# A two-layer attention-bias kernel in ten regions of rows instead of eleven, with other store and load pieces

## The chip, the cores and the metric

The kernel runs on one core of a Trainium2 chip. The metric is the device time of one execution in microseconds (us). Lower is better. The engines are called as in the profile: PE (TensorE), DVE (VectorE), ACT (ScalarE), POOL (GpSimd) and SP (SyncE, which here only issues DMAs).

## The reference

The input x has 16 heads of 1024 rows (t) by 1024 columns (s), all float32. The output has the same shape. Two layers are applied one after the other:

```python
x = x + bias.transpose(2, 0, 1)[None]                 # bias[t, s, head]
ret = einsum('BGMTS,GMN->BGNTS', x, w + eye)
ret += einsum('BGITS,BTGIM->BGMTS', einsum('BGMTS,BTGIM->BGITS', x, qw1), qw2)
ret += einsum('BGMTS,BSGIM->BGITS', x, kw1) followed by kw2
ret += x * qdd (by row and head) + x * kdd (by column and head)
```

The bias is a small network of the distance of row and column: a logarithm of the distance, divided by one of the row's position, goes through 32 hidden units with a relu and then through a 32 x 16 matrix. In the second layer the 16 heads of each point (t, s) are mixed by a 16 x 16 matrix that is the sum of a part that depends on the row t ("a", from w, qw1, qw2, qdd) and a part that depends on the column s ("b", from kw1, kw2, kdd).

## The kernel before

The 1024 rows are cut into 128 tiles of 8 rows. A tile holds all 1024 columns and all 16 heads: 8 blocks of 128 columns by 16 heads make the 128 partitions, and each partition has 8 x 128 = 1024 numbers, so a tile is 512 KB. Tiles are grouped into regions (`REGION_TILES`): one of 6 tiles, nine of 13, one of 5, eleven in all. The text calls them region 0 to region 10. SBUF has three "homes" of 13 tiles each. The biased x of region k lies in home k mod 3, and its mixed output goes into the home behind it in that ring ((k + 2) mod 3), from which it is stored. The x of region k + 2 is loaded into the home of region k's output, one tile further on, and so each piece of that load waits until the store of the tiles lying there is out (`out_done`). The last tile of a region's load falls into the first tile of the next home and waits for the first store piece there.

A region has two phases on PE. First come 16 column steps (`b_columns`, L772): each takes 8 columns of every block and multiplies all rows of the region by the column's matrices. A step has 16 matmuls with 64 x 64 weights and as many columns as the region has rows (104 for 13 tiles). For regions of up to 8 tiles (`NARROW_TILES`) a step has 32 matmuls with 32 x 32 weights instead (48 or 40 columns). ACT and DVE copy the sums out of PSUM (`take_b`, L528 and L641) in turn, in region 0 ACT alone; PSUM holds two such steps. Then come the row tiles (`a_rows`, L759), one for each tile of the region, with 16 matmuls of 128 columns each; DVE adds their results to the copied sums (`finish_tile`, L651). Each matmul of an order is two instructions in the trace.

Between these steps the bias of the NEXT region is made, one tile at a time, spread evenly over the steps from step 4 on (`bias_step`). For a tile POOL makes the hidden values (L462), ACT the relu (L501), PE the product (`bias_tile`, L789), and DVE (L677, L671) and ACT (L512) add it to x, for which they wait for the load of that tile's piece (`x_landed`). In the first 64 tiles this takes one pass of POOL and ACT for each tile; in the last 64 it takes two. The text calls regions 1 to 3 light and regions 4 to 8 heavy (in region 4 half of the next region's tiles take two passes). POOL also spreads the row matrices of each tile out into the weights that PE needs (L439), in a ring of four tiles. They come from `mats_in`, which SP loads for four tiles at a time (`load_mats_a`, L333).

Before region 0 the kernel loads its constants, makes the bias of region 0's own tiles, builds the column matrices on DVE (`compact("b")`) and sends them through DRAM into `mats_b`. After the last tile of that bias DVE builds the row matrices (`compact("a")`, L298 to L606), PE transposes them after the fourth column step (`TURN_AT`), and SP writes them to DRAM and reads them back (L359, L333). A table of scales for later rows goes to DRAM, too (`late_scales`, L380). The scratch for all this lies in parts of the homes that are not yet used, so some loads have to come after it.

SP issues all loads and half of the stores from one queue, in an order that is written out in the program: in region k, at tile T, first the row matrices that are due, then the last piece of x for region k + 1, then the store piece that ends there (waiting until DVE has finished its last tile), then a piece of x for region k + 2 (at T = 7, 10 and 12). The remaining pieces for region k + 1 stand at the start of region k. ACT issues the other half of the stores, in two portions at the two steps after a piece's last tile. Each piece of a load or of a store is one DMA for each of the 8 blocks (8 loads on SP; 4 stores on SP and 4 on ACT). The pieces are in `LOAD_PIECES` and `STORE_PIECES`, in tiles.

## Time and profile before

| | us |
|---|---|
| median of 3 runs | 897.41 (889.36 to 899.29) |
| the profiled execution | 896.75 |
| its span, from the first to the last instruction | 894.9 |
| around the span | 1.85 |
| mean granted TensorE clock | 0.894 |

Engine times of the page are sums over the span, and a share of busy time says little where the stages have different limits. The stages are best read from windows that are cut at the first column step of each region; the timeline gives these times, 46.3 us for region 0 and 839.2 us for region 10 being the first and the last.

### The profile page before, as it was taken

Reading aid. Unit: us, or ns where it says so; the run is one execution under the profiler, and the core shown is the slowest. Engines: PE = TensorE matmul, PEld = TensorE weight load, DVE = VectorE, ACT = ScalarE, POOL = GpSimd, SP = SyncE. Lnnn points to the kernel's source line nnn. Section 1 sums busy time; section 2 is a strip of 40 time slices with the busy share of each in tenths; the row PEclk is TensorE's granted clock in tenths of the full one; section 3 lists DMA queues with packets and bytes.
Section 4 is the critical chain, followed back from the end, with each engine's and each line's share of the span. In section 5 each row is a group of like instructions: output and inputs, shape, how many; then the busy total and the mean of one; then the engine's idle time right before and its main releaser. Section 6 shows DMA issues by size and latency. Waiting matters only on the chain. (4 is left out here: it accounts for less than half of the span.)

```text
span 894.9 us, 28881 instructions
## 1 busy us (share of the span) xinstructions
PE 699.0 (78%) x12836; PEld 586.1 (65%) x12836; DVE 481.0 (54%) x629; ACT 395.8 (44%) x428; POOL 513.4 (57%) x463
## 2 busy tenths in 40 slices
PE   0466767986998798696699859969988896699764
PEld 0254566875887688585577657756866685589664
DVE  7667625863693595475346625653475365335412
ACT  5756536544743663563245325433543453232000
POOL 4524823734475257368558937985898588635300
PEclk9876978988998899899899979998999999799857
DMA  6578559597778979877885888589859897843905
GB/s 129 137 169 147 132 145 205 128 227 169 181 185 208 208 149 223 213 159 150 189 195 125 201 185 188 113 185 215 183 123 184 180 198 151 212 111 73 258 7 118
DMA packets 302936, 148.98 MB, mean 166 GB/s; under 512 B 31964, under 2 KB 298588, under 8 KB 302812
## 3 DMA queue, kind: packets, MB, share of 16 engines
q1 hardware_dynamic: 232928, 113.56, 57.5%
q10 hardware_dynamic: 69884, 33.58, 16.3%
q8 instruction: 101, 1.65, 0.8%
q14 instruction: 23, 0.19, 0.1%
HBM read 77.61 MB, written 69.47 MB: 164 GB/s over the span
## 5 line engine op out<-in xcount | busy, mean ns | idle before, releaser
L462 POOL TENSOR_TENSOR hidden<-log_table,row_scale 128x1024 f32<-128x1024 f32 x192 | 364.3, 1913 | 218.3 <-PE bias L789 210.4
L772 PEld LDWEIGHTS main<-homes,mats_b 64*64 64x64 f32 (+1 forms) x6656 | 316.9, 189 | 150.3 <-ACT homes L528 65.1
L772 PE MATMUL main<-homes,mats_b 64*64 64x104 f32 (+2 forms) x6656 | 332.5, 274 | 106.1 <-ACT homes L528 50.7
L501 ACT ACTIVATE hidden<-hidden,b_col 128x1024 f32<-128x1024 f32 x192 | 221.0, 1152 | 259.6 <-POOL hidden L462 187.6
L759 PEld LDWEIGHTS main<-homes,mats_a 64*64 64x64 f32 x4096 | 239.2, 136 | 51.3 <-issue 37.4
L759 PE MATMUL main<-homes,mats_a 64*64 64x128 f32 x4096 | 256.0, 279 | 5.2 <-POOL mats_a L439 3.5
L439 POOL TENSOR_TENSOR mats_a<-mats_in,own_block 128x256 f32<-128x256 f32 x256 | 153.6, 655 | 143.0 <-DMA mats_in<-a_mats 112.9
L651 DVE TENSOR_TENSOR homes<-main,homes 128x1024 f32<-128x1024 f32 x128 | 156.7, 1225 | 59.4 <-PE main L759 54.3
L641 DVE COPY homes<-main 128x832 f32<-128x832 f32 (+1 forms) x80 | 77.7, 971 | 192.1 <-PE main L772 189.2
L789 PE MATMUL bias<-hidden,w_blocks 64*32 64x256 f32 (+1 forms) x2048 | 120.4, 528 | 58.0 <-ACT hidden L501 46.4
L677 DVE SCALAR_TENSOR_TENSOR homes<-bias,b_col,homes 64x256 f32<-64x256 f32 x256 | 122.9, 480 | 76.7 <-DMA homes<-in_x 52.8
L528 ACT ACTIVATE homes<-main 128x832 f32<-128x832 f32 (+2 forms) x96 | 73.4, 764 | 141.2 <-PE main L772 125.9
L671 DVE SCALAR_TENSOR_TENSOR homes<-bias,b_col,homes 128x512 f32<-128x512 f32 x128 | 90.3, 747 | 68.0 <-PE bias L789 58.2
L512 ACT ACTIVATE homes<-homes,b_col 64x512 f32<-64x512 f32 x128 | 89.9, 754 | 63.5 <-DMA homes<-in_x 52.3
L789 PEld LDWEIGHTS bias<-hidden,w_blocks 64*32 64x32 f32 x2048 | 24.8, 108 | 79.4 <-issue 60.2
L298 DVE TENSOR_TENSOR homes<-homes 128x2048 f32<-128x2048 f32 x4 | 12.3, 3123 | 0.1
L719 PE MATMUL bias<-relu_b,w_blocks 64*32 64x1 f32 x4 | 0.3, 191 | 13.7 <-DVE w_blocks L626 13.7
L719 PEld LDWEIGHTS bias<-relu_b,w_blocks 64*32 64x32 f32 x4 | 0.2, 136 | 13.6 <-issue 13.6
L495 ACT ACTIVATE mats_b<-zero_col 128x8192 f32<-128x8192 f32 x1 | 7.0, 7012 | 0.0
L712 PE MATMUL main<-homes 128*128 128x128 f32 x32 | 5.6, 350 | 0.6 <-DVE homes L606 0.6
L712 PEld LDWEIGHTS main<-homes 128*128 128x128 f32 x32 | 5.0, 183 | 1.5 <-issue 0.8
L601 DVE TENSOR_TENSOR homes<-homes 128x2048 f32<-128x2048 f32 x2 | 4.6, 2292 | 0.1
(40 smaller groups left out, 33.0 us busy)
## 6 DMA issues: line engine op xcount, KB each, us to landing
homes<-in_x SPq DMA_DIRECT2D x224, 192.0 KB, 6.2
out_mixed<-homes SPq DMA_DIRECT2D x108, 192.0 KB, 4.8
out_mixed<-homes ACTq DMA_DIRECT2D x108, 192.0 KB, 5.4
out_mixed<-homes SPq DMA_DIRECT2D x88, 128.0 KB, 3.5
out_mixed<-homes ACTq DMA_DIRECT2D x88, 128.0 KB, 3.6
homes<-in_x SPq DMA_DIRECT2D x160, 64.0 KB, 4.4
homes<-in_x SPq DMA_DIRECT2D x80, 128.0 KB, 4.5
mats_in<-a_mats SPq DMA_DIRECT2D x128, 64.0 KB
```

The source lines that it names most:

```text
L439: spread_half = nc.gpsimd.tensor_tensor(bass.AP(mats_a, w % A_RING_UNITS * A_UNIT + q * GP, [[A_RING_UNITS * A_UNIT, P], [GS, H], [1, GS], ...
L462: nc.gpsimd.tensor_tensor(hidden_tile(u, g).rearrange("p (j b s) -> p j b s", b=2, s=W), bass.AP(log_table, t0 - SLOTS * W * g, [[2 * TABL ...
L501: nc.scalar.activation(hidden_tile(u, g), hidden_tile(u, g), ACT.Relu, bias=b1_col[:, 0:1])\
L512: add = nc.scalar.activation(y_rows(high_half, k, T, b), x_rows(high_half, k, T, b), ACT.Identity, bias=b2_col[high_half, 1:2])
L528: nc.scalar.activation(mixed_columns(k, C), column_sums(k, C), ACT.Copy)\
L641: dve.tensor_copy(mixed_columns(k, C), column_sums(k, C)).then_inc(main_taken[b_tile(k, C) % 2], 1)
L651: dve.tensor_tensor(at, main[:, i % 2, :], at, ALU.add).then_inc(main_taken[i % 2], 1)
L671: add = dve.scalar_tensor_tensor(out=y_rows(whole, k, T, b), in0=falling(u, b), scalar=b2_col[:, 0:1], in1=x_rows(whole, k, T, b), op0=ALU ...
L677: add = dve.scalar_tensor_tensor(out=y_rows(low_half, k, T, b)[:, some], in0=falling_part(u, part, b), scalar=b2_col[low_half, 0:1], in1=x ...
L759: mm = pe.matmul(main[of_wide(g), i % 2, j * W:(j + 1) * W], a_weights(g, w, j), y_row(k, T, g, j), start=True, stop=True)
L772: mm = pe.matmul(main[at, i % 2, j * W:j * W + REGION_TILES[k] * ROWS], b_weights(at, C * ROWS + j), y_column(k, at, C * ROWS + j), start= ...
L789: mm = pe.matmul(bias[quadrant(q), u % 2, b * BANK:b * BANK + n * W], w2_blocks[of, :], rows[:, b, part * n:(part + 1) * n, :], start=True ...
```

## The change

The regions become one of 11 tiles and nine of 13, so there are ten, region 0 to region 9. With 11 tiles region 0 takes the wide column steps, and no region takes the narrow ones. A full region's stores go out in six pieces of 1, 2, 3, 3, 2, 2 tiles instead of five of 2, 3, 3, 3, 2, and the last region has a list of its own. The x of a full region comes in pieces of 1, 2, 3, 3, 3, 1 tiles instead of 1, 3, 3, 3, 2, 1. The scratch moves into other parts of the homes, and the order of SP's start changes with it. DVE makes the late scales one bias tile sooner.

```diff
+SCRATCH_FROM = 9
-REGION_TILES = (6,) + (13,) * 9 + (5,)
+REGION_TILES = (11,) + (13,) * 9
...
-STORE_PIECES = {6: (2, 2, 2), 13: (2, 3, 3, 3, 2), 5: (2, 1, 1, 1)}
-STORE_SEMS = max(len(sizes) for sizes in STORE_PIECES.values())
-LOAD_PIECES = {6: (1, 2, 3), 13: (1, 3, 3, 3, 2, 1), 5: (1, 4)}
+STORE_PIECES = {11: (2, 3, 3, 3), 13: (1, 2, 3, 3, 2, 2)}
+LAST_STORES = (2, 3, 3, 2, 1, 1, 1)
+STORE_SEMS = len(LAST_STORES)
+LOAD_PIECES = {11: (1, 2, 4, 4), 13: (1, 2, 3, 3, 3, 1)}
...
-            return STORE_PIECES[REGION_TILES[k]]
+            return LAST_STORES if k == REGIONS - 1 else STORE_PIECES[REGION_TILES[k]]
+
+        def loads_ahead(k):
+
+            return len(load_pieces(k)) - (REGION_TILES[k] == HOME_TILES)
...
             for i in range(3):
                 load_x(1, i)
             save_mats("a")
-            load_x(1, 3)
             sp.wait_ge(mats_out["a"], 2 * DMA)
             for v in range(A_RING):
                 load_mats_a(v)
-            load_x(1, 4)
             sp.wait_ge(tables_made, 3)
             sp.dma_start(late_scales, scale_late).then_inc(scales_out, DMA)
-            loaded = [3, 5] + [0] * (REGIONS - 2)
+            sp.wait_ge(scales_out, DMA)
+            for i in range(3, loads_ahead(1)):
+                load_x(1, i)
+            loaded = [loads_ahead(0), loads_ahead(1)] + [0] * (REGIONS - 2)
...
-                        if T == piece_start(store_pieces(k), i + 1) - 1 - (i == 4 and k < REGIONS - 1):
+                        if T == piece_start(store_pieces(k), i + 1) - 1 - (REGION_TILES[k] == HOME_TILES and i == len(store_pieces(k)) - 1 and k < REGIONS - 1):
                             store_upper(k, i)
...
-                    if k == 0 and T == 3:
+                    if k == 0 and T == 2:
                         invert(scale_late)
```

Three places show how instructions move. In a row, the last numbers before the count are the shape; for loads and stores 16x8x128 is one tile of one block, 16x24x128 is three tiles, and a count of 8 (loads) or 4 (stores) is one piece.

SP at the start, from the first load of region 1's x on, before:

```order
L325 DMA homes<-in_x 16x8x128 x8
L325 DMA homes<-in_x 16x24x128 x16
L359 DMA a_mats<-homes 128x32x32 x2
L325 DMA homes<-in_x 16x24x128 x8
L333 DMA mats_in<-a_mats 32x1x512 x8
L325 DMA homes<-in_x 16x16x128 x8
L380 DMA late_scales<-homes 128x512
L276 DMA out_mixed<-homes 16x16x128 x4
```

and now:

```order
L332 DMA homes<-in_x 16x8x128 x8
L332 DMA homes<-in_x 16x16x128 x8
L332 DMA homes<-in_x 16x24x128 x8
L366 DMA a_mats<-homes 128x32x32 x2
L340 DMA mats_in<-a_mats 32x1x512 x8
L385 DMA late_scales<-homes 128x512
L332 DMA homes<-in_x 16x24x128 x16
L283 DMA out_mixed<-homes 16x16x128 x4
```

The two pieces of x that hold tiles 6 to 11 of region 1 now stand behind the late scales, and wait until these have landed in DRAM.

SP in a full light region, at the same phase of the row matrices (region 2 before), from its first store on:

```order
L276 DMA out_mixed<-homes 16x16x128 x4
L333 DMA mats_in<-a_mats 32x1x512 x4
L276 DMA out_mixed<-homes 16x24x128 x4
L325 DMA homes<-in_x 16x8x128 x8
L333 DMA mats_in<-a_mats 32x1x512 x4
L276 DMA out_mixed<-homes 16x24x128 x4
L325 DMA homes<-in_x 16x8x128 x8
L276 DMA out_mixed<-homes 16x24x128 x4
L325 DMA homes<-in_x 16x24x128 x8
L333 DMA mats_in<-a_mats 32x1x512 x4
L276 DMA out_mixed<-homes 16x16x128 x4
L325 DMA homes<-in_x 16x24x128 x16
```

and now (region 1):

```order
L283 DMA out_mixed<-homes 16x8x128 x4
L283 DMA out_mixed<-homes 16x16x128 x4
L340 DMA mats_in<-a_mats 32x1x512 x4
L283 DMA out_mixed<-homes 16x24x128 x4
L332 DMA homes<-in_x 16x8x128 x8
L340 DMA mats_in<-a_mats 32x1x512 x4
L332 DMA homes<-in_x 16x8x128 x8
L283 DMA out_mixed<-homes 16x24x128 x4
L283 DMA out_mixed<-homes 16x16x128 x4
L332 DMA homes<-in_x 16x16x128 x8
L340 DMA mats_in<-a_mats 32x1x512 x4
L283 DMA out_mixed<-homes 16x16x128 x4
```

Ahead of the first one-tile load (the last tile of the next region) there are now 12 stores and 6 stored tiles instead of 8 and 5. The second piece of x for the region after that has 2 tiles instead of 3 and comes behind 20 stores instead of 16; the third piece, of 3 tiles, follows the last row shown in both.

PE at the end of the program, before:

```order
L789 MATMUL bias<-hidden,w_blocks 32x512 x8
L759 MATMUL main<-homes,mats_a 64x128 x96
L789 MATMUL bias<-hidden,w_blocks 32x512 x8
L759 MATMUL main<-homes,mats_a 64x128 x16
L772 MATMUL main<-homes,mats_b 32x40 x512
L759 MATMUL main<-homes,mats_a 64x128 x80
L67 UNCONDITIONAL_BRANCH
```

and now:

```order
L767 MATMUL main<-homes,mats_a 64x128 x32
L797 MATMUL bias<-hidden,w_blocks 32x512 x8
L767 MATMUL main<-homes,mats_a 64x128 x16
L780 MATMUL main<-homes,mats_b 64x104 x256
L767 MATMUL main<-homes,mats_a 64x128 x208
L69 UNCONDITIONAL_BRANCH
```

The narrow region of 512 small matmuls and 5 row tiles at the end is gone; the program now ends with a full region of 16 wide column steps and 13 row tiles with no bias between them.

## Rows read from the trace of the kernel before

**Rows 1.** The page, part 1: busy time, share of the span, instructions.

```profile
PE 699.0 (78%) x12836; PEld 586.1 (65%) x12836; DVE 481.0 (54%) x629; ACT 395.8 (44%) x428; POOL 513.4 (57%) x463
```

**Rows 2.** Windows: stretch, length, busy PE, PEld, DVE, ACT, POOL, clock, DMA, GB/s.

```profile
46.30:119.70 73.40, 45.63 (x1442) 35.02 (x1442) 46.29 (x68) 42.38 (x57) 35.95 (x33) 0.78 0.71 150
119.70:350.30 230.60, 199.62 (x3409) 176.78 (x3409) 144.84 (x220) 119.48 (x141) 115.62 (x114) 0.90 0.82 185
350.30:771.50 421.20, 352.04 (x5682) 285.05 (x5684) 214.33 (x247) 182.64 (x177) 304.53 (x252) 0.94 0.80 176
518.30:609.80 91.50, 71.94 (x1140) 58.01 (x1138) 42.44 (x47) 37.25 (x36) 68.48 (x58) 0.91 0.79 169
771.50:839.20 67.70, 60.81 (x1012) 55.21 (x1008) 31.13 (x31) 17.52 (x18) 30.96 (x33) 0.92 0.62 143
839.20:894.90 55.70, 30.83 (x1186) 29.07 (x1184) 11.28 (x14) 3.50 (x8) 4.72 (x8) 0.65 0.43 99
```

**Rows 3.** Timeline, start of the program (start, length, engine, line, idle before).

```profile
39.49 1.11 PE L789 MATMUL bias<-hidden,w_blocks 64*32 64x256 f32 x16 [1.47 <-ACT hidden L501]
...
42.88 4.49 DVE L298 TENSOR_TENSOR homes<-homes 128x2048 f32<-128x2048 f32 x2
...
46.26 4.55 PE L772 MATMUL main<-homes,mats_b 32*32 32x48 f32 x231 [5.66 <-DMA mats_b<-b_mats]
...
52.06 0.37 DVE L606 TENSOR_TENSOR homes<-homes 128x128 f32<-128x128 f32 x1
...
54.70 1.12 PE L772 MATMUL main<-homes,mats_b 32*32 32x48 f32 x64 [0.24 <-ACT homes L520]
```

**Rows 4.** DMA issues by line: count, KB of each, median us to landing.

```profile
homes<-in_x SPq DMA_DIRECT2D x224, 192.0 KB, 6.2
out_mixed<-homes SPq DMA_DIRECT2D x108, 192.0 KB, 4.8
...
a_mats<-homes SPq DMA_DIRECT2D x2, 512.0 KB, 10.9
out_mixed<-homes SPq DMA_DIRECT2D x12, 64.0 KB, 2.4
...
late_scales<-homes SPq DMA_DIRECT2D x1, 256.0 KB, 4.6
```

**Rows 5.** The page, part 5: groups of instructions (busy, mean ns of one, idle before).

```profile
L462 POOL TENSOR_TENSOR hidden<-log_table,row_scale 128x1024 f32<-128x1024 f32 x192 | 364.3, 1913 | 218.3 <-PE bias L789 210.4
...
L677 DVE SCALAR_TENSOR_TENSOR homes<-bias,b_col,homes 64x256 f32<-64x256 f32 x256 | 122.9, 480 | 76.7 <-DMA homes<-in_x 52.8
```

**Rows 6.** Timeline, region 10 and the end.

```profile
866.21 2.36 PE L772 MATMUL main<-homes,mats_b 32*32 32x40 f32 x128 [1.12 <-issue]
...
870.80 11.73 PE L759 MATMUL main<-homes,mats_a 64*64 64x128 f32 x160
...
882.58 1.23 DVE L651 TENSOR_TENSOR homes<-main,homes 128x1024 f32<-128x1024 f32 x1 [0.59 <-PE main L759]
```

**Rows 7.** Timeline, region 2: a stall, column steps, row tiles.

```profile
221.69 5.81 PE L772 MATMUL main<-homes,mats_b 64*64 64x104 f32 x64 [8.28 <-ACT homes L528]
...
228.03 3.77 PE L772 MATMUL main<-homes,mats_b 64*64 64x104 f32 x64
...
262.84 3.85 PE L759 MATMUL main<-homes,mats_a 64*64 64x128 f32 x64
```

**Rows 8.** Timeline of SP, early in region 3.

```profile
295.34 20.39 SPq L325 DMA_DIRECT2D homes<-in_x  x24
```

**Rows 9.** Timeline, the start of region 6 (518.3 us).

```profile
524.47 2.34 POOL L439 TENSOR_TENSOR mats_a<-mats_in,own_block 128x256 f32<-128x256 f32 x4 [8.51 <-DMA mats_in<-a_mats]
```

**Rows 10.** Waits of ACT and of PE, 119.7 to 434.2 and 350.3 to 771.5 us.

```profile
ACT homes L512 <- DMA homes<-in_x: 39.5, 8, 8.9
...
PE bias L789 <- ACT hidden L501: 39.0, 25, 5.0
PE main L772 <- ACT homes L528: 24.6, 3, 9.0
```

More of the change, by code:

```diff
@@ L95, in build @@
         thr_col = sb("thr_col", [P, 3])
-        spare_0 = homes[:, (REGION_TILES[0] + 1) * COLS:HOME_TILES * COLS]
-        spare_2 = homes[:, (2 * HOME_TILES + REGION_TILES[0]) * COLS:HOMES * HOME_TILES * COLS]
-        comp = {"a": spare_2[:, 0:2048], "b": spare_2[:, 2048:4096]}
-        term = {"a": spare_0[:, 0:2048], "b": spare_2[:, 4096:6144]}
-        turned = term
-        first = {"a": spare_2[:, 6144:6400], "b": spare_2[:, 6400:6656]}
-        second = {"a": spare_2[:, 6656:6912], "b": spare_2[:, 6912:7168]}
-        diag = {"a": spare_0[:, 2048:2176], "b": spare_0[:, 2176:2304]}
-        w_eye = spare_0[:, 2304:2560]
-        ident = spare_0[:, 2560:2688]
-        w2_rows = spare_0[:, 2688:2704]
-        own_halves = spare_0[:, 2704:2704 + GROUPS * GS]
-        scale_late = spare_0[:, 2816:2816 + PART]
+        spare_1 = homes[:, (HOME_TILES + SCRATCH_FROM) * COLS:2 * HOME_TILES * COLS]
+        home_2 = homes[:, 2 * HOME_TILES * COLS:HOMES * HOME_TILES * COLS]
+        spare_2 = home_2[:, REGION_TILES[0] * COLS:HOME_TILES * COLS]
+        comp = {"a": spare_2[:, 0:2048], "b": home_2[:, 0:2048]}
+        term = {"a": spare_1[:, 0:2048], "b": home_2[:, 2048:4096]}
+        turned = term
+        first = {"a": spare_1[:, 2048:2304], "b": home_2[:, 4096:4352]}
+        second = {"a": spare_1[:, 2304:2560], "b": home_2[:, 4352:4608]}
+        diag = {"a": spare_1[:, 2560:2688], "b": home_2[:, 4608:4736]}
+        w_eye = spare_1[:, 2688:2944]
+        ident = spare_1[:, 2944:3072]
+        w2_rows = spare_1[:, 3072:3088]
+        own_halves = spare_1[:, 3088:3088 + GROUPS * GS]
+        scale_late = spare_1[:, 3104:3104 + PART]
         main = ctx.enter_context(nc.psum_tensor("main", [P, 2, COLS], F32))
@@ L364, in _ @@
             sp.dma_start(w_eye, w.rearrange("g m n -> g (m n)").partition_broadcast(P)).then_inc(weights_in["a"], DMA)
-            load_x(0, 1)
-            load_x(0, 2)
+            for i in range(1, loads_ahead(0)):
+                load_x(0, i)
             save_mats("b")
@@ L377, in _ @@
                 load_mats_a(v)
-            load_x(1, 4)
             sp.wait_ge(tables_made, 3)
             sp.dma_start(late_scales, scale_late).then_inc(scales_out, DMA)
-            loaded = [3, 5] + [0] * (REGIONS - 2)
+            sp.wait_ge(scales_out, DMA)
+            for i in range(3, loads_ahead(1)):
+                load_x(1, i)
+            loaded = [loads_ahead(0), loads_ahead(1)] + [0] * (REGIONS - 2)
             for k in range(REGIONS):
-                while k + 1 < REGIONS and loaded[k + 1] < min(5, len(load_pieces(k + 1))):
+                while k + 1 < REGIONS and loaded[k + 1] < loads_ahead(k + 1):
                     load_x(k + 1, loaded[k + 1])
@@ L397, in _ @@
                         load_mats_a(v)
-                    if k + 1 < REGIONS and len(load_pieces(k + 1)) > 5 and T == min(6, REGION_TILES[k] - 4):
-                        load_x(k + 1, 5)
+                    if k + 1 < REGIONS and REGION_TILES[k + 1] == HOME_TILES and T == min(6, REGION_TILES[k] - 4):
+                        load_x(k + 1, loads_ahead(k + 1))
                     for i in range(len(store_pieces(k))):
-                        if T == piece_start(store_pieces(k), i + 1) - 1 - (i == 4 and k < REGIONS - 1):
+                        if T == piece_start(store_pieces(k), i + 1) - 1 - (REGION_TILES[k] == HOME_TILES and i == len(store_pieces(k)) - 1 and k < REGIONS - 1):
                             store_upper(k, i)
                     if k + 2 < REGIONS and (T in AHEAD or k == 0 and T == REGION_TILES[0] - 1) \
-                            and loaded[k + 2] < len(load_pieces(k + 2)):
+                            and loaded[k + 2] < loads_ahead(k + 2):
                         load_x(k + 2, loaded[k + 2])
```

## The prediction

> **What bounds the kernel now.** The page comes first. No engine is full: PE, the busiest, works for 78% of the span [rows 1], so the time must be read by stages. For that I cut the span where the timeline shows each region's first column step, and asked for the windows [rows 2]. The reader should divide length by tiles. Start-up takes 46.3 us. Region 0 takes 73.4 us for 6 tiles, regions 1 to 3 take 230.6 for 39, regions 4 to 8 take 421.2 for 65, region 9 takes 67.7 for 13, and region 10, with the last stores, 55.7 for 5. These six add up to the span of 894.9. A tile costs 5.2 to 7.0 us in a full region, but 12.2 in region 0 and 11.1 in region 10. The short regions are dear, because 16 column steps are done however many rows share them.
>
> What a step costs is read from the timeline. Two wide steps (64 instructions) take 3.77 us, 1.885 each, and two row tiles 3.85, 1.925 each [rows 7]. Two narrow steps of region 10 take 2.36, 1.18 each, but then 1.12 pass in which PE waits for nothing the profile names [rows 6]; with such pauses its column phase lasts from 839.2 to 870.8, 31.6 us. Sixteen wide steps are 16 x 1.885 = 30.2. So 5 tiles pay as much for columns as 13 do.
>
> Then the waits. In the light regions ACT and DVE wait for x that has not landed: ACT loses 39.5 us in 8 such waits between 119.7 and 434.2 [rows 10], and one of them holds PE for 8.28 us in region 2 [rows 7]. In the heavy regions POOL is late, because the row matrices land late: 8.51 us at the start of region 6 [rows 9]. PE then waits for the hidden values, 39.0 us in 25 waits, and for ACT's copies, 24.6 us in 3 [rows 10]. SP issues both kinds of load from one queue, so both waits hang on how far SP lags behind PE.
>
> **The end.** Region 10 goes, and the last region has 13 tiles and no bias beside it. Columns: 30.2 us, plus 2 for ACT, which issues two stores of the region before ahead of its first copy (an estimate: two issues of 0.85 [rows 8]). Rows: 13 x 1.925 = 25.0. The tail after PE's last row tile was 894.9 - 882.5 = 12.4 [rows 2, 6]; the last store pieces were 2, 1, 1, 1 tiles and are still 2, 1, 1, 1, so I keep it. Sum 69.6, where regions 9 and 10 took 123.4 together.
>
> **The start.** Eleven tiles of bias stand ahead of region 0 instead of six. PE's sixth came at 39.49 after 1.47 us idle, so one tile takes 1.47 + 1.11 = 2.58 [rows 3]. The eleventh comes at 39.5 + 5 x 2.58 = 52.4. From the sixth to the start of the row matrices on DVE 3.4 us passed (42.88 - 39.49), so region 0 can start at about 55.8. Before, it waited for the column matrices until 46.26 [rows 3]; they queue behind five more tiles of x now, 2.5 MB, but have 9.5 us more to land. If they take longer still, the start slips by as much.
>
> DVE needs 52.43 - 42.88 = 9.55 us for the row matrices, and from their end to the next column step 2.3 us passed [rows 3]: column step 4 starts at 67.7. Twelve wide steps of 88 columns are at most 12 x 1.885 = 22.6, and seven bias tiles lie between them. The seventh needs tile 6 of region 1, whose load now stands behind the row matrices and the late scales. That chain: matrices out at 68.7, landed 10.9 later [rows 4], read back in about 6 (8 issues), 86; scales out, 4.6 [rows 4] and the issue, 92; 8 loads and 6.2 to land [rows 4], about 102. DVE makes these scales after the third bias tile now, at column step 7 (before after the fourth, at step 8). They are ready when the matrices are read back, so this move saves nothing here, and at most the wait for one bias addition. ACT holds PE until 104, some 8 us later than its own work would. From there DVE has 10 row tiles of 1.23 [rows 6] and six bias additions of 4 x 0.48 = 1.92 [rows 5], and one of each is left over from the wait: 27 us, and the one-tile load behind the fourth row tile's store ends at the same time. Region 1 starts at 132. Bounds: 124 without the wait, 142 if every load is as late as a_mats was. Before it was 119.7, so five tiles cost 12.3 us more.
>
> **The full light regions (1 to 3).** Their work does not change; the pieces do. Each has four more stores on SP and four more on ACT. Issues cost 20.39 / 24 = 0.85 us in the busy stretch [rows 8], so four are 3.4. Against this the first store starts a row tile sooner (about 2.5), when SP is waiting for it. The second piece of x has a third fewer bytes and so lands up to 2.5 us sooner, but the third piece now begins with tile 3 instead of tile 4. That tile is used two steps and a bias tile earlier, over 2 x 1.885 = 3.8 us, while its piece lands 1 us later to 2.6 sooner. The wait at tile 1 becomes a wait at tile 3. Bounds: the waits vanish (8.28 off in region 2), or 5 us come on top in each. I take 2 each, since the queue is the same and the last data that a step needs come no sooner: 230.6 + 6 = 236.6.
>
> A rule of the Trainium skill speaks against such pieces. The rows show 2.4 us to landing for a store DMA of 64 KB and 4.8 for one of 192 KB [rows 4], which is 1.2 per 64 KB and 1.2 that does not shrink. The Trainium skill ("DMA: Bandwidth & Descriptors", section "Anatomy of one DMA") states a fixed part of about 2.0 us for each DMA, and "Measured" there advises batches of 1 MiB. Were 2.0 paid once more in each of the nine full regions, the sum would be 18 us higher; the trace has the next issue 0.85 behind, beside that latency.
>
> **The heavy regions (4 to 8).** There are still five, and 64 tiles with two passes, but region 4 now has 12 of them to make instead of 7. POOL's second pass is 1.91 us [rows 5], so this costs 0 to 9.5; I take 5, since half of the region is bound by POOL. Row matrices due at tiles 7, 9, 10 and 11 stand behind four more stores, 0 to 3.4 each; they delay POOL only where it already waits. I take 4 for all. 421.2 + 9 = 430.2. Bounds: 2 less in each if the earlier first store helps, or all as long as region 6, 91.5 [rows 2].
>
> **Sum.** 132.0 + 236.6 + 430.2 + 69.6 = 868.4, plus the 1.85 around the span: 870.3, called 870. The profiled execution took 896.75 and the median of the runs is 897.41, so both stand for the same; 870 is 3.0% less.
>
> **Rivals.**
>
> *The finer pieces dissolve the waits for x (0.13).* The second piece lands in time and the third as well. For it: the first store leaves sooner, while SP stands idle. Against it: the third piece holds a tile that is needed sooner. ACT's waits of 39.5 us lie in about four regions [rows 10], 9.9 in each, and PE, which runs two steps ahead, loses less. Were 6 saved in each light region instead of 2 lost, the time would be 870 - 24 = 846.
>
> *The pieces cost what the short region gives (0.20).* Each region pays in series: the light ones 5 instead of 2, the heavy ones 3.4 each, 17 instead of 4. That is 9 + 13 more: 892, no change. For it: SP lags PE already, and the DMA engines are 0.80 to 0.82 busy in these stretches [rows 2]. Against it: the bytes are the same. The rule of the Trainium skill above would end here, at 888.
>
> *The row matrices come late in every heavy region (0.10).* Region 6, with its wait, took 91.5 us; the other four average (421.2 - 91.5) / 4 = 82.4 [rows 2]. If four more issues ahead of `load_mats_a` put all five regions there and add 3.4, they take 5 x 94.9 = 474.5 instead of 430.2: 870 + 44 = 914, slower. For it: the matrices are asked for only about two row tiles ahead of their use. Against it: the matrices fall due at another tile in each region, and only some of these lie behind more stores than before. It decides once the matrices land later than those two row tiles, about 6 us, in each region.
>
> **How the numbers follow.** My forecast has 0.57, with a range of its own of 856 to 884 (the start's bounds, 2 us per light region either way). A measurement of this kernel can tell about 1% from no change, here 888 to 906. Faster by more: 0.56 + 0.13, and a third of the 0.20, 0.75. Within 1%: the rest of it, 0.14. Slower: 0.10 and a little, 0.11. The range of 846 to 896 leaves out the slower rival and about half of the first.
>
> **What would show it.** Right: no PE instructions with 32 x 32 weights for columns; region 1 starting between 124 and 142; the last region, with the tail, at 67 to 73; the light regions' waits for x moved from tile 1 to tile 3. Wrong: region 1 later than 145 (the start pays for what the end saves), heavy regions of 90 or more with POOL waiting for `mats_in` longer than before (the third rival), or light regions under 72 (the first).

## The result and the profile after

The changed kernel took 860.77 us (median of 4 runs, 859.05 to 868.05), the kernel before, beside it, 898.35 (889.36 to 902.84). One of its four runs, that of 902.84, counts as slow, and the ratio leaves it out. The ratio is 0.963, with a 95% interval of 0.953 to 0.973: 3.7% faster. The forecast was 870 with a range of 846 to 896. The profiled execution took 861.78, of which 860.0 is the span and 1.78 lies around it.

The page, part 1, of the kernel after, against [rows 1]:

```profile
PE 680.8 (79%) x11300; PEld 574.0 (67%) x11300; DVE 474.9 (55%) x621; ACT 395.4 (46%) x420; POOL 512.9 (60%) x463
```

PE has 1536 instructions less. A narrow region's 16 column steps are 1024 instructions, a wide region's 512; two narrow regions go and one wide comes. But PE's work fell by 18.2 us only, and the span by 34.9: about half of the gain was not PE's work. In the rows shown line numbers are 8 higher than before for the computing engines (column steps L780, row tiles L767, bias product L797), and 7 higher for SP (store L283, load of x L332, row matrices L340).

The windows of the kernel after, cut as in [rows 2] (stretch, length, busy PE, PEld, DVE, ACT, POOL, clock, DMA, GB/s):

```profile
0.00:57.20 57.20, 14.34 (x198) 5.53 (x198) 39.38 (x70) 42.89 (x44) 31.12 (x29) 0.82 0.71 153
57.20:141.10 83.90, 63.65 (x1088) 55.74 (x1088) 53.41 (x75) 46.35 (x57) 41.79 (x43) 0.89 0.73 160
141.10:384.30 243.20, 199.35 (x3408) 175.99 (x3408) 144.88 (x220) 119.99 (x142) 114.59 (x112) 0.89 0.79 179
384.30:791.00 406.70, 350.67 (x5680) 284.56 (x5682) 211.86 (x237) 179.23 (x171) 313.42 (x259) 0.96 0.80 181
791.00:860.00 69.00, 52.81 (x932) 52.14 (x928) 25.34 (x22) 6.91 (x8) 11.98 (x20) 0.92 0.58 138
```

Read down the lengths. Start-up and region 0 now take 141.1 us instead of 119.7. The light regions take 243.2 instead of 230.6, the heavy ones 406.7 instead of 421.2, and the end 69.0 instead of 67.7 + 55.7 = 123.4. That is +21.4, +12.6, -14.5 and -54.4, in sum -34.9. The second number of a row, PE's work, hardly moved in the light and heavy regions (199.62 to 199.35, 352.04 to 350.67). What changed there is time in which PE stood still: 31.0 to 43.9 us and 69.2 to 56.0.

The end, in the timeline of the kernel after, against [rows 6]:

```profile
791.00 3.79 PE L780 MATMUL main<-homes,mats_b 64*64 64x104 f32 x64
...
796.12 25.23 PE L780 MATMUL main<-homes,mats_b 64*64 64x104 f32 x448 [1.32 <-ACT homes L536]
...
821.18 16.48 PE L767 MATMUL main<-homes,mats_a 64*64 64x128 f32 x288
...
839.39 7.47 PE L767 MATMUL main<-homes,mats_a 64*64 64x128 f32 x128 [1.73 <-POOL mats_a L447]
```

The columns take 821.18 - 791.00 = 30.2 us with the wait of 1.32, the 13 row tiles 25.7 (821.18 to 846.86) with the wait of 1.73, and 13.1 remain for the last stores.

The start, in the timeline of PE, ACT and DVE:

```profile
105.32 1.37 ACT L520 ACTIVATE homes<-homes,b_col 64x512 f32<-64x512 f32 x2 [9.12 <-DMA homes<-in_x]
...
107.61 5.83 PE L767 MATMUL main<-homes,mats_a 64*64 64x128 f32 x64 [8.73 <-ACT homes L536]
...
139.09 1.97 DVE L685 SCALAR_TENSOR_TENSOR homes<-bias,b_col,homes 64x256 f32<-64x256 f32 x4 [8.45 <-DMA homes<-in_x]
...
141.12 1.14 PE L780 MATMUL main<-homes,mats_b 64*64 64x104 f32 x10 [9.23 <-DVE homes L685]
```

There are two stalls. Tile 6 of region 1 arrives at 105.3, and PE stands still for 8.73 us. The region's last tile, the one-tile piece, arrives at 139.1, and PE stands still for 9.23. SP's queue in the same stretch says why:

```profile
112.58 3.60 SPq L283 DMA_DIRECT2D out_mixed<-homes  x4
116.22 3.16 SPq L340 DMA_DIRECT2D mats_in<-a_mats  x4
121.00 4.66 SPq L283 DMA_DIRECT2D out_mixed<-homes  x4
125.70 4.55 SPq L340 DMA_DIRECT2D mats_in<-a_mats  x4
130.30 5.74 SPq L332 DMA_DIRECT2D homes<-in_x  x8
```

The last row is the one-tile load. Right ahead of it stand row matrices, 4.55 us of issues, and ahead of these a store, for which SP had waited until 121.00, when DVE was done with tile 4.

The light regions, in PE's own timeline of regions 1 to 3, against [rows 7] (the rows of regions 1 and 2 with a stall on x inside the region):

```profile
166.36 5.00 PE L780 MATMUL main<-homes,mats_b 64*64 64x104 f32 x64 [6.92 <-ACT homes L536]
...
242.27 4.70 PE L780 MATMUL main<-homes,mats_b 64*64 64x104 f32 x64 [6.43 <-ACT homes L536]
256.98 5.56 PE L780 MATMUL main<-homes,mats_b 64*64 64x104 f32 x64 [5.12 <-ACT homes L536]
```

Where region 2 had one stall of 8.28 us [rows 7], it has two now, 6.43 for the second piece of x (tile 1) and 5.12 for the third (tile 3); region 3 likewise has 4.58 and 3.62.

The waits of SP and of PE in the heavy regions (384.3 to 791.0), against [rows 10]. Each row gives the wait in sum, how many times it came, and the longest. Of before, the first of these waits was 56.9 us in 10 times (its row stands with the experiments):

```profile
SPq L283 <- DVE homes L659: 39.9, 12, 10.9
...
PE bias L797 <- ACT hidden L509: 38.5, 29, 3.7
...
PE main L780 <- ACT homes L536: 16.4, 4, 8.6
```

SP waits for DVE 17 us less, though it has more stores to wait for. This is not idle time of the bottleneck, but everything queued behind such a wait goes out later, and that is what the experiments are about.

### The profile page after: what moved, and what is told of

The parts are those of the page before. It is cut to its first block and busy times, and to the rows that moved or that the text cites. A ratio compares the mean times of both kernels' runs of the same rounds, so it can differ in the third digit from the quotient of the medians.

```text
span 860.0 us, 25839 instructions
## 1 busy us (share of the span) xinstructions
PE 680.8 (79%) x11300; PEld 574.0 (67%) x11300; DVE 474.9 (55%) x621; ACT 395.4 (46%) x420; POOL 512.9 (60%) x463
## 5 line engine op out<-in xcount | busy, mean ns | idle before, releaser
L780 PEld LDWEIGHTS main<-homes,mats_b 64*64 64x64 f32 x5120 | 308.9, 204 | 107.2 <-ACT homes L536 62.8
L780 PE MATMUL main<-homes,mats_b 64*64 64x104 f32 (+1 forms) x5120 | 320.8, 283 | 68.1 <-ACT homes L536 44.7
L767 PEld LDWEIGHTS main<-homes,mats_a 64*64 64x64 f32 x4096 | 236.0, 134 | 59.5 <-issue 46.9
L767 PE MATMUL main<-homes,mats_a 64*64 64x128 f32 x4096 | 252.6, 277 | 17.3 <-ACT homes L536 8.7
L797 PE MATMUL bias<-hidden,w_blocks 64*32 64x256 f32 (+1 forms) x2048 | 117.0, 514 | 65.4 <-ACT hidden L509 54.9
L649 DVE COPY homes<-main 128x832 f32<-128x832 f32 x72 | 73.7, 1024 | 148.6 <-PE main L780 148.3
L536 ACT ACTIVATE homes<-main 128x832 f32<-128x832 f32 (+1 forms) x88 | 73.6, 840 | 97.5 <-PE main L780 96.3
L797 PEld LDWEIGHTS bias<-hidden,w_blocks 64*32 64x32 f32 x2048 | 24.8, 107 | 89.7 <-issue 63.2
L305 DVE TENSOR_TENSOR homes<-homes 128x2048 f32<-128x2048 f32 x4 | 12.3, 3122 | 0.1
L727 PEld LDWEIGHTS bias<-relu_b,w_blocks 64*32 64x32 f32 x4 | 0.2, 136 | 13.6 <-issue 13.6
L528 ACT ACTIVATE homes<-main 128x1024 f32<-128x1024 f32 x4 | 3.9, 1021 | 1.9 <-PE main L720 1.9
```

The source lines that it names most:

```text
L536: nc.scalar.activation(mixed_columns(k, C), column_sums(k, C), ACT.Copy)\
L649: dve.tensor_copy(mixed_columns(k, C), column_sums(k, C)).then_inc(main_taken[b_tile(k, C) % 2], 1)
L767: mm = pe.matmul(main[of_wide(g), i % 2, j * W:(j + 1) * W], a_weights(g, w, j), y_row(k, T, g, j), start=True, stop=True)
L780: mm = pe.matmul(main[at, i % 2, j * W:j * W + REGION_TILES[k] * ROWS], b_weights(at, C * ROWS + j), y_column(k, at, C * ROWS + j), start= ...
L797: mm = pe.matmul(bias[quadrant(q), u % 2, b * BANK:b * BANK + n * W], w2_blocks[of, :], rows[:, b, part * n:(part + 1) * n, :], start=True ...
```

## Experiments

All ratios are to the kernel before, run beside each on the same chip. The names of the kernels say what they hold: ten or eleven regions, and old or new pieces of stores and loads. "The changed kernel" and "after" are the same.

### Regions and pieces apart

Ten regions with both old lists:

```diff
-STORE_PIECES = {11: (2, 3, 3, 3), 13: (1, 2, 3, 3, 2, 2)}
+STORE_PIECES = {11: (2, 3, 3, 3), 13: (2, 3, 3, 3, 2)}
-LOAD_PIECES = {11: (1, 2, 4, 4), 13: (1, 2, 3, 3, 3, 1)}
+LOAD_PIECES = {11: (1, 2, 4, 4), 13: (1, 3, 3, 3, 2, 1)}
```

> Ten regions with the old pieces in the full regions (stores 2, 3, 3, 3, 2; loads 1, 3, 3, 3, 2, 1). Theory 'regions': the smaller number of regions carries the whole gain and the new pieces cost a little in the light regions; then the light regions fall from 243 back to about 231 us, the heavy ones stay near 407, and the time is about 848 to 855. Theory 'pieces': the heavy regions are shorter because of the new pieces; then they go back to 421 to 430 us, and the time is 865 to 875. Theory 'phases': the heavy regions are shorter because the row matrices fall due at other tiles now that region 0 has 11 tiles; then they stay near 407 with either pieces, and only the light ones tell the pieces apart.

Measured: 859.60 us (858.36 to 863.32), ratio 0.962 (0.957 to 0.967).

Only the first of the two lines (old stores, new loads):

> Ten regions, new loads (1, 2, 3, 3, 3, 1), old stores (2, 3, 3, 3, 2). Theory 'regions' or 'phases': four stores fewer on SP per region ahead of the second piece of x; light regions 235 to 240 us, time 853 to 860. Theory 'pieces': the one-tile first store is what frees SP earlier, so without it the time is above 865.

Measured: 863.47 (861.14 to 868.51), ratio 0.966 (0.960 to 0.973).

Only the second (new stores, old loads):

> Ten regions, new stores (1, 2, 3, 3, 2, 2), old loads (1, 3, 3, 3, 2, 1). If the new loads cost in the light regions, because their third piece begins a tile sooner, the time falls by 3 to 8 us under 861; if they help, because the second piece lands sooner, it rises to 865 to 870.

Measured: 859.14 (855.56 to 874.01), ratio 0.959 (0.953 to 0.965).

The kernel before with the new pieces in its full regions:

```diff
-STORE_PIECES = {6: (2, 2, 2), 13: (2, 3, 3, 3, 2), 5: (2, 1, 1, 1)}
+STORE_PIECES = {6: (2, 2, 2), 13: (1, 2, 3, 3, 2, 2), 5: (2, 1, 1, 1)}
-LOAD_PIECES = {6: (1, 2, 3), 13: (1, 3, 3, 3, 2, 1), 5: (1, 4)}
+LOAD_PIECES = {6: (1, 2, 3), 13: (1, 2, 3, 3, 3, 1), 5: (1, 4)}
...
-if T == piece_start(store_pieces(k), i + 1) - 1 - (i == 4 and k < REGIONS - 1):
+if T == piece_start(store_pieces(k), i + 1) - 1 - (i == 5 and k < REGIONS - 1):
```

> The kernel before with its eleven regions, and the new pieces in its full regions. Theory 'regions': no gain, 895 to 905 us (my sum: 6 us more in the light and 4 more in the heavy regions). Theory 'pieces': the heavy regions fall by some 15 us as they did with the whole change, and the time is 880 to 888. Theory 'phases': the heavy regions stay near 421.

Measured: 890.65 (887.69 to 894.28), ratio 0.996 (0.993 to 0.999).

The stages of all of these and of the later ones, from the timelines (first column step of each region), in us of the profiled execution:

| kernel | region 1 starts | regions 1 to 3 | regions 4 to 8 | from region 9 on |
|---|---|---|---|---|
| before | 119.7 | 230.6 | 421.2 | 123.4 |
| eleven_new_both | 118.4 | 233.9 | 412.0 | 121.9 |
| ten_old_both | 137.6 | 237.9 | 414.1 | 68.5 |
| ten_old_stores | 143.2 | 237.6 | 412.8 | 67.9 |
| ten_old_loads | 141.4 | 240.6 | 405.9 | 68.6 |
| after | 141.1 | 243.2 | 406.7 | 69.0 |
| after_again | 141.8 | 239.3 | 406.3 | 68.0 |
| two_three | 140.8 | 243.3 | 418.1 | 68.2 |
| first_two | 142.2 | 234.7 | 407.2 | 68.0 |
| first_two_again | 142.1 | 232.3 | 405.1 | 68.6 |
| first_two_old_loads | 139.1 | 232.9 | 412.5 | 68.3 |
| early_last | 133.7 | 249.9 | 408.3 | 71.0 |
| split_start | 144.8 | 238.9 | 405.2 | 69.3 |
| early_split | 136.1 | 245.8 | 402.4 | 70.8 |

What follows: the new regions alone carry the whole gain (0.962 with old pieces, 0.963 with new). The pieces alone are worth 0.4% in eleven regions and nothing that can be told in ten. A stage moves by up to 4 us between two profiles of one kernel (the two rows of the changed kernel), so only differences beyond that count. By this the cost of the pieces in the light regions is not shown (3.3 us in eleven regions, 5.3 or 1.4 in ten, by which profile of the changed kernel is taken), and their gain in the heavy ones is (9.2 in eleven, 7.4 or 7.8 in ten). Of the two lists it is the stores that do it: with old stores the heavy regions take 413 to 414, with the new ones 406 to 407, whichever loads go with them. (With the stores 2, 2, 3, 2, 2, 2 further down the loads do seem to matter there, 412.5 against 407.2 and 405.1.)

None of the theories came as it was put. The time of ten_old_both lies above what 'regions' gave and below 'pieces', and its heavy regions take 414.1, neither 407 nor 421; eleven_new_both is faster than 'regions' and slower than 'pieces' gave; ten_old_stores and ten_old_loads fall between their alternatives. The heavy regions gain about 7 us by the new regions and 7 to 9 by the stores.

One rival is untested. With the short regions the narrow column steps went, too, and in the kernel before PE stood 13.9 us in region 0 and 12.1 in region 10 in pauses inside those steps (the last section shows where they come from). No run keeps eleven regions and gives the short ones wide steps, so how much of the gain comes from one region less, and how much from the narrow steps, is not told apart.

The waits of SP in the heavy regions, before, in eleven regions with new pieces, and in ten with old ones, a row from each:

```profile
SPq L276 <- DVE homes L651: 56.9, 10, 10.1
```

```profile
SPq L276 <- DVE homes L651: 36.3, 11, 7.9
```

```profile
SPq L283 <- DVE homes L659: 57.3, 10, 13.7
```

With old stores SP waits 57 us for DVE, with new ones 36 and 40, in ten regions as in eleven. PE's own waits do not say as plainly where the gain arrives: between the old and new pieces of ten regions PE's wait for the hidden values falls from 43.0 to 38.5, between those of eleven it is the wait for ACT's copies that falls, from 24.6 to 19.0.

### The stall at the start

Theory: the one-tile load comes late because it stands behind what is due by tile 6, so issued earlier it would bring region 1 forward, and the whole kernel with it. Rival: SP sets the pace for regions 0 and 1 together, and what is won at region 1 is lost again at region 2.

```diff
-if k + 1 < REGIONS and REGION_TILES[k + 1] == HOME_TILES and T == min(6, REGION_TILES[k] - 4):
+if k + 1 < REGIONS and REGION_TILES[k + 1] == HOME_TILES and T == (2 if k == 0 else 6):
```

> The changed kernel with one move: in region 0 SP issues the last one-tile piece of region 1's x at tile 2 instead of tile 6. It removes most of PE's wait of 9.2 us ahead of region 1. Theory 'SP's order of work sets the pace': the second piece of region 2's x lands no sooner, since SP has the same loads and stores ahead of it, and PE waits for it longer in region 1; region 1 starts 6 to 8 us sooner, region 2 starts within 2 us of where it did, and the time stays at 859 to 862. Theory 'every wait of PE counts': the time falls by 6 to 8 us, to 853 to 855.

Measured: 863.30 (861.12 to 865.19), ratio 0.961 (0.956 to 0.965). Region 1 did start earlier. From the timeline of early_last, the starts of regions 1 and 2 and the stall between:

```profile
133.70 9.19 PE L780 MATMUL main<-homes,mats_b 64*64 64x104 f32 x160 [1.28 <-DVE homes L685]
...
165.98 5.21 PE L780 MATMUL main<-homes,mats_b 64*64 64x104 f32 x64 [9.24 <-ACT homes L536]
...
218.29 3.91 PE L780 MATMUL main<-homes,mats_b 64*64 64x104 f32 x64 [1.19 <-DVE homes L685]
```

and of the changed kernel, the start of region 2:

```profile
218.28 10.04 PE L780 MATMUL main<-homes,mats_b 64*64 64x104 f32 x160 [2.79 <-DVE homes L685]
```

The stall of 9.23 us shrank to 1.28, and region 1 began 7.4 us sooner. Region 2 began where it had, to 0.01 us. In between the wait at tile 1 grew from 6.92 to 9.24, since its piece still comes at SP's own time, and PE waited 4.84 us for DVE's copies at 152.79, where the changed kernel has no such wait. SP issues without a stop from 121.0 to 181.0 us in the changed kernel and from 121.2 to 179.9 in early_last; that piece is among these loads. The rival holds.

The other stall at the start, for tile 6, was attacked by splitting region 1's pieces otherwise and sending four of them ahead of the row matrices:

```diff
+return (1, 2, 3, 2, 4, 1) if k == 1 else LOAD_PIECES[REGION_TILES[k]]
...
-for i in range(3):
+for i in range(4):
     load_x(1, i)
 save_mats("a")
```

> The changed kernel with region 1's x in pieces of 1, 2, 3, 2, 4, 1 tiles. The fourth piece (tiles 6 and 7) then lies ahead of the scratch and is issued before the row matrices go out, instead of behind the late scales. PE's wait of 8.7 us in region 0 for tile 6 goes or moves to tile 8. The first store of region 0 leaves sooner, and SP's whole queue with it, so both theories expect a gain: 4 to 7 us, 854 to 857, if tile 8's piece lands in time; none if it lands as late as tile 6's did (106 us) and the wait is 6 us or more there.

Measured: 863.68 (860.14 to 866.25), ratio 0.962 (0.957 to 0.968). From its timeline, PE in region 0 and the start of region 1:

```profile
120.81 3.68 PE L767 MATMUL main<-homes,mats_a 64*64 64x128 f32 x32 [11.78 <-POOL mats_a L447]
...
144.85 10.78 PE L780 MATMUL main<-homes,mats_b 64*64 64x104 f32 x160 [8.49 <-DVE homes L685]
```

The stall for tile 6 is gone, and a longer one stands in its place: row matrices now hold PE for 11.78 us. They are issued at 114.8, in the changed kernel at 116.2: SP has no stop from 100.4 until they are out at 117.4 and can't send them much sooner, and PE is there earlier. Neither theory's gain came. Both edits together:

> Both moves. Theory 'SP's order': the same as split_start alone, within 2 us. Theory 'every wait of PE counts': the sum of the two, 845 to 850.

Measured: 862.05 (856.88 to 865.64), ratio 0.959 (0.953 to 0.965). Three orders of the start end within 3 us of each other and of the changed kernel, and region 2 starts at 218.3, 221.6 and 219.3 in their profiles (218.3 and 218.4 in the two of the changed kernel). This fits a start that is set by how much SP has to send, where the order only picks the engine that shows it. No run takes DMAs off SP in this stretch, so that much is a reading and not shown.

### Which property of the new stores pays

The new list differs from the old in a first store of one tile, in one piece more, and in where its pieces end. The first theory was that the one-tile store wakes SP sooner. A list with a first store of two tiles tells it apart:

```diff
-STORE_PIECES = {11: (2, 3, 3, 3), 13: (1, 2, 3, 3, 2, 2)}
+STORE_PIECES = {11: (2, 3, 3, 3), 13: (2, 2, 3, 2, 2, 2)}
```

> The changed kernel with six store pieces of 2, 2, 3, 2, 2, 2 tiles in full regions: as many stores, but the first is of two tiles and so leaves SP one row tile later. Theory 'the one-tile first store wakes SP sooner': in the heavy regions SP's waits for DVE go back from 40 to about 57 us, the row matrices due at tiles 8 and 9 are issued 11 us or more after they are due instead of 7 to 9, and regions 4 to 8 take 412 to 418 us instead of 407. Theory 'smaller pieces': they stay near 407.

Measured: 855.13 (853.97 to 855.24), ratio 0.951 (0.947 to 0.955). The theory falls: the heavy regions stay at 407, and the light ones give back 8.5 us (why is open). SP's waits for DVE in the heavy regions did go back in part, to 46.0 us, and the heavy regions did not follow. The next theories: smaller pieces pay as such, or what counts is which tile's store is the last ahead of the row matrices. (2, 3, 2, 2, 2, 2) has six pieces like the new list but ends its second at tile 4, as the old one does:

```diff
-STORE_PIECES = {11: (2, 3, 3, 3), 13: (1, 2, 3, 3, 2, 2)}
+STORE_PIECES = {11: (2, 3, 3, 3), 13: (2, 3, 2, 2, 2, 2)}
```

> Ten regions, new loads, six store pieces of 2, 3, 2, 2, 2, 2 tiles. SP's first two store pieces are as before the change, so after the last store for which SP has to wait for DVE (tile 4) it has 24 issues ahead of the row matrices due at tile 8, as with the old stores; with 2, 2, 3, 2, 2, 2 it has these 24 too, but waits last at tile 3. Theory 'what is queued behind SP's last wait': the matrices due at tile 8 of region 4 are issued 10 us or more after they are due, regions 4 to 8 take 411 to 415 us, and the time is about 860 to 864. Theory 'smaller pieces': they are issued about 7 us after, the heavy regions stay near 407, and the time is 854 to 857.

Measured: 870.21 (863.87 to 872.33), ratio 0.970 (0.964 to 0.975). Six pieces, and the heavy regions take 418.1, more than with the old five. So smallness is not it. The queue of SP in region 4, up to the row matrices due at tile 8 (the last row of each), shows what differs. With the old stores in ten regions:

```profile
425.96 2.55 SPq L340 DMA_DIRECT2D mats_in<-a_mats  x4
431.98 4.74 SPq L283 DMA_DIRECT2D out_mixed<-homes  x4
436.76 5.79 SPq L332 DMA_DIRECT2D homes<-in_x  x8
442.60 3.92 SPq L283 DMA_DIRECT2D out_mixed<-homes  x4
446.56 6.63 SPq L332 DMA_DIRECT2D homes<-in_x  x8
453.23 2.84 SPq L340 DMA_DIRECT2D mats_in<-a_mats  x4
```

In the changed kernel:

```profile
435.08 3.39 SPq L340 DMA_DIRECT2D mats_in<-a_mats  x4
439.93 2.87 SPq L283 DMA_DIRECT2D out_mixed<-homes  x4
442.84 13.03 SPq L332 DMA_DIRECT2D homes<-in_x  x16
455.91 3.14 SPq L340 DMA_DIRECT2D mats_in<-a_mats  x4
```

In first_two:

```profile
425.73 7.61 SPq L283 DMA_DIRECT2D out_mixed<-homes  x8
433.39 3.39 SPq L340 DMA_DIRECT2D mats_in<-a_mats  x4
436.82 5.12 SPq L332 DMA_DIRECT2D homes<-in_x  x8
441.99 3.68 SPq L283 DMA_DIRECT2D out_mixed<-homes  x4
445.71 6.29 SPq L332 DMA_DIRECT2D homes<-in_x  x8
452.04 2.50 SPq L340 DMA_DIRECT2D mats_in<-a_mats  x4
```

All three send 12 stores of this region ahead of these matrices (the first four or eight, at 423.36 and 427.78, stand above the rows shown); the number is the same. With the old stores SP stops at 428.51 (425.96 + 2.55) until tile 4 is done, 3.5 us, and then has 24 DMAs to issue, 21.3 us, among them the store that ends at tile 7. In the changed kernel the last store ahead ends at tile 5, SP stops for 1.5 us, and 20 DMAs follow, 16.0 us.

In first_two the first row hides a stop, since it holds two pieces: the first is out at 428.5, and the second, which ends at tile 3, begins at 430.5, 2.1 us later. From there on SP has 24 DMAs as with the old stores, and four row matrices, 21.5 us, but it is let go one tile sooner. two_three stops for tile 4 until 440.9 and then has 24 DMAs, too.

What POOL feels is in its timeline of the same place: the first matrices that it has to wait for. With the old stores:

```profile
460.19 2.34 POOL L447 TENSOR_TENSOR mats_a<-mats_in,own_block 128x256 f32<-128x256 f32 x4 [8.02 <-DMA mats_in<-a_mats]
```

in the changed kernel:

```profile
464.63 2.34 POOL L447 TENSOR_TENSOR mats_a<-mats_in,own_block 128x256 f32<-128x256 f32 x4 [6.35 <-DMA mats_in<-a_mats]
```

and in two_three:

```profile
469.24 2.34 POOL L447 TENSOR_TENSOR mats_a<-mats_in,own_block 128x256 f32<-128x256 f32 x4 [8.18 <-DMA mats_in<-a_mats]
```

This is the wait of [rows 9], one region earlier. All kernels with ten regions, with the time from the end of tile 7 on DVE to the first issue of these matrices, POOL's wait for them, and the length of the heavy regions:

| kernel | stores of a full region | issued after tile 7 | POOL's wait | regions 4 to 8 |
|---|---|---|---|---|
| ten_old_both | 2, 3, 3, 3, 2 | 13.5 | 8.02 | 414.1 |
| ten_old_stores | 2, 3, 3, 3, 2 | 14.4 | 8.97 | 412.8 |
| two_three | 2, 3, 2, 2, 2, 2 | 13.6 | 8.18 | 418.1 |
| after | 1, 2, 3, 3, 2, 2 | 10.0 | 6.35 | 406.7 |
| after_again | 1, 2, 3, 3, 2, 2 | 9.5 | 4.75 | 406.3 |
| ten_old_loads | 1, 2, 3, 3, 2, 2 | 9.5 | 5.71 | 405.9 |
| early_last | 1, 2, 3, 3, 2, 2 | 9.8 | 5.38 | 408.3 |
| split_start | 1, 2, 3, 3, 2, 2 | 12.4 | 7.98 | 405.2 |
| early_split | 1, 2, 3, 3, 2, 2 | 10.0 | other wait last | 402.4 |
| first_two | 2, 2, 3, 2, 2, 2 | 9.9 | 5.33 | 407.2 |
| first_two_again | 2, 2, 3, 2, 2, 2 | 10.3 | 5.85 | 405.1 |
| first_two_old_loads | 2, 2, 3, 2, 2, 2 | 9.7 | 4.96 | 412.5 |

With a store that ends at tile 4 the matrices are issued 13.5 us or later after tile 7 and POOL waits 8 us or more; with the other lists it is 9.5 to 10.3 and 4.75 to 6.35, but for split_start. In eleven regions the new pieces cut the same wait of region 6 from 8.51 to 4.82. Four regions later, where the row matrices fall due at the same tiles again, the wait is 4.34, 4.22 and 2.71 in the three that end a store at tile 4, and 2.0 or less in all others. So stores that let SP go earlier, or leave it less to send, bring these matrices sooner: this much is shown, with the one exception.

That the 7 to 9 us of all heavy regions are made of this wait and others like it is not shown, and two rows speak against it: split_start waits long and has short heavy regions, first_two_old_loads the other way round. POOL's waits for row matrices sum up to 41.7 us in the heavy regions of ten_old_both, and to 42.8 and 37.2 in the two profiles of the changed kernel, so the sum does not tell. What makes the heavy regions shorter with the new stores stays open.

The same first-two stores with old loads, and the two best candidates once more:

> Stores of 2, 2, 3, 2, 2, 2 with the old loads 1, 3, 3, 3, 2, 1. The two pairs so far say that the loads make no difference beyond noise (859.6 against 863.5 with the old stores, 859.1 against 860.8 with the new): then this takes 852 to 856. If the new loads are what makes these stores fast, it takes 858 or more.

> The changed kernel again, on the same chip as the next: 859 to 864.

> The version with stores of 2, 2, 3, 2, 2, 2 again: 853 to 857 if its lead over the changed kernel is one of the kernel and not of the chip it ran on; within 3 us of after_again if not.

Measured: 854.21 (852.23 to 859.90), ratio 0.954 (0.948 to 0.960), for first_two_old_loads; 861.48 (857.16 to 869.23), ratio 0.962 (0.957 to 0.966), for the changed kernel again; 852.29 (847.07 to 854.95), ratio 0.950 (0.946 to 0.955), for first_two. The last two intervals don't meet. With stores of 2, 2, 3, 2, 2, 2 tiles the kernel beats both: 9 us (1.1%) under the changed kernel, 44 under the one before. The pieces of x make no difference that can be told (852.3 and 854.2, ratios overlapping).

## Why the prediction was right, and where it was not

The forecast was faster by 3.0%, and it was 3.7%. The likeliest case came, and the three rivals did not: the waits for x did not dissolve (ACT's eight waits between 141.1 and 460.7 are 55.5 us, where [rows 10] had 39.5), the pieces did not eat the gain, and the longest heavy region of the changed kernel's profile took 88.4 us (460.7 to 549.1), where the third rival needed 94.9 in each. Of the signs, region 1 started at 141.1 (124 to 142), the end took 69.0 (67 to 73), and no column step has 32 x 32 weights; that the waits for x move from tile 1 to tile 3 did not come, since both are there. Step by step, against the sum of 132.0 + 236.6 + 430.2 + 69.6:

- *The end, 69.6 against 69.0: right, by its own steps.* Columns 30.2 and rows 25.7 came near what was worked out (30.2 and 25.0). But the 30.2 hold the wait for ACT's copy, 1.3 instead of the 2 that the sum had beside them (14 steps in 25.23 are 1.80 each, not 1.885), and the 25.7 hold a wait of 1.73 for row matrices that the sum did not have. The tail was 13.1 instead of 12.4.
- *The start, 132.0 against 141.1: mis-sized by 9.* Region 0 began at 57.2 (55.8 forecast), tile 6 landed at 105.3 (102; from 92 on eight issues at the sum's own 0.85 and 6.2 to land give 105), and PE was held to 107.6 (104). That is 3.6 of the 9. The step that failed is "the one-tile load behind the fourth row tile's store ends at the same time". The step left out the row matrices due at the same tile, which SP issues first: 4.55 us, from 125.70. And the store ahead ends with tile 4, the fifth row tile, done at 121.0. I counted what the load is said to stand behind, and not the queue row by row. early_last shows that this cost nothing in the end: without the stall the kernel was as slow, because the next region took the time back.
- *The light regions, 236.6 against 243.2: too low.* "The wait at tile 1 becomes a wait at tile 3" failed: both are there now, 6.43 and 5.12 in region 2. The 6 us for the pieces were 5.3 or 1.4, by the profile, which noise may hold. The rest, 230.6 to 237.9 with old pieces, comes from the ten regions, for which the sum had nothing: over the three regions PE's waits for ACT's copies grow from 19.1 to 22.1 us (9.52 at tile 1 of region 1 in ten_old_both, 4.47 before), and those for POOL's row matrices from 2.8 to 8.3. Both loads come from SP, which leaves region 0 with more to send; that this is the reason is likely and not shown.
- *The heavy regions, 430.2 against 406.7: wrong in sign, by 23.5.* Two terms failed. The 4 us for row matrices that "stand behind four more stores, 0 to 3.4 each" counted DMAs. In ten_old_stores and the changed kernel the same number of stores, 12, stands ahead of the matrices due at tile 8 of region 4, and the finer list brings them sooner (14.4 and 10.0 us after tile 7), with 20 DMAs after SP's last stop instead of 24. Instead of +4 the stores gave -7 to -9 in these regions; what the rest of that is made of stays open. And the 5 us for region 4's two-pass tiles: POOL's work in these regions did grow, from 304.53 to 313.42 us, by 8.9 of the 9.5 that I allowed. But region 4 got shorter, 83.9 to 79.0 us in ten_old_both. Before, PE stalled there for a tile of x, because ACT waited for it ahead of a copy. This is the row of PE, and below it ACT's wait in region 4 of before (sum, times, longest):

```profile
374.69 4.80 PE L772 MATMUL main<-homes,mats_b 64*64 64x104 f32 x64 [7.68 <-ACT homes L528]
```

```profile
ACT homes L512 <- DMA homes<-in_x: 8.3, 1, 8.3
```

In the kernel ACT takes part in the addition to x only for one-pass tiles; for two-pass tiles DVE adds alone (`add_const_bias`). With ten regions all tiles of region 5 but its first take two passes. So in region 4 of ten_old_both it is DVE that waits for the x, and ACT has no such wait:

```profile
DVE homes L679 <- DMA homes<-in_x: 10.1, 1, 10.1
```

The x comes no sooner (23.1 us into the region, 22.1 before), but ACT's copies go on, and PE's longest wait there is one of 3.60 for hidden values. The prediction took 5 of 9.5 "since half of the region is bound by POOL", and asked only what would hide POOL's extra work, not which wait that work would replace.

For the regions alone the terms are 12.3 - 53.8 + 5 = -36.5, and ten_old_both measured 36 us less (895.75 to 859.60). That is luck, a good sum of wrong parts: its stages moved by +17.9, +7.3, -7.1 and -54.9. The pieces were forecast at +10 and gave nothing that can be told in sum, about -7 in the heavy regions and a light-region cost within the noise.

The Trainium skill states the 2.0 us for each DMA ("DMA: Bandwidth & Descriptors", "Anatomy of one DMA") for DMAs that GpSimd issues; those here are issued by SP and ACT. Paid once more in each full region, it would have made the pieces 18 us dearer. In eleven regions they took 5 us off (0.993 to 0.999). Landing did get no quicker per byte: the page's DMA issues of the kernel after have

```profile
out_mixed<-homes SPq DMA_DIRECT2D x84, 192.0 KB, 5.0
...
out_mixed<-homes SPq DMA_DIRECT2D x108, 128.0 KB, 4.1
```

so 128 KB take four fifths of the time of 192 KB. A part that does not shrink is there (an estimate from these two rows: 5.0 - 3 x 0.9 = 2.3 us), but the next DMA is issued 0.7 to 1.2 us behind, and the price did not show in the kernel's time.

## What to carry to other kernels

In a queue that issues in order and waits, don't price an added DMA by its issue alone: look for the last stop that the queue makes ahead of what is urgent, which event ends it, and how much is queued behind it. Here that told when the row matrices came; it did not tell what the kernel's time would do. A wait for data costs the bottleneck nothing while it sits on an engine that the bottleneck does not need soon: DVE's 10.1 us for x left PE alone, ACT's 8.3 did not. A stall removed early in a program is worth nothing if the same queue sets the next stage's start; one removed stall (early_last: 7.4 us won at region 1, none at region 2) shows it at once. A phase whose cost does not shrink with its tile count is best paid for by full tiles, and the gain is the short tile's time less what it makes the start longer.

## What was not expected of the hardware

The narrow column steps paid for pauses in which PE waits for nothing that the profile names: 1.12 us after two steps of 2.36 [rows 6]. They make 12.1 us of region 10's 31.6 for columns, and 13.9 us of region 0. The trace shows what PE waits for. Its DMA queues hold one of kind "instruction"; before and after it moved (packets, MB, share):

```profile
q8 instruction: 101, 1.65, 0.8%
```

```profile
q8 instruction: 89, 1.46, 0.8%
```

That is 16 KB for each packet. The 12 packets less go with 1536 matmuls and 1536 weight loads less, so a packet is 256 of PE's instructions. From the second pause of region 10 on there are 128 matmuls from one to the next, which with their weight loads are 256 instructions, and of the fourteen pauses of 0.5 us or more in the two narrow regions thirteen end 1.2 to 1.5 us after such a packet has landed (the packets are in the trace). So PE is through with its instructions before the next ones are there (no run changes this alone; the reading rests on the times and the counts). Packets come 3.5 to 4.3 us apart there, for two narrow steps that PE works through in 2.36; 128 matmuls of wide steps take 7.5 us. The changed kernel has no such pause in its first and last region: 448 instructions in one row of 25.23 us. So 104 columns took less time (30.2 us) than 40 (31.6).

The granted clock differs, too, 0.60 in region 10's column phase (839.2 to 870.8) and 1.00 in that of the last region now. After 845 us, behind the first pause, it was at the lower of its two levels (0.50, 1.2 GHz). But the clock does not make the pauses: the first steps of region 0 run at 0.50 without one (177 matmuls in 3.50 us), and the pause of 1.69 us ahead of 58.35 came at 1.00.

SP's time for an issue is no constant: four stores took 3.60 to 4.66 us in the start's rows and eight loads 5.74, four row matrices 3.16 to 4.55. That is 0.7 to 1.2 us each, beside the 0.85 that the sum used.
